# A two-layer latent attention kernel: the second layer's packed queries come through memory, first keys and turned maxima are rearranged

## The chip, the cores and the metric

One NeuronCore of one Trainium2 chip runs the whole program. The metric is the device time of one execution in microseconds (us). The kernel before took 1229.85 us as the median of three executions (1229.53, 1229.85 and 1231.4).

## What is computed

A Perceiver-like network of two layers. The latents `x` are 128 rows of 256; the context is 12,544 rows of 192. Each layer is a cross attention from the latents to the context, a small attention or feed-forward among the latents, and a mixture of experts. What the change touches is the cross attention, in both layers:

```python
q = (query @ Wq + bq)   # 128 x (heads*d); layer 0: 8 heads of 64, no bias; layer 1: 16 heads of 16
k = (key @ Wk + bk)     # 12544 x (heads*d)
v = (value @ Wv + bv)
attn = softmax(q k^T * d**-0.5, axis=-1)
out = attn @ v, then @ Wo + bo
x = x + out
```

with `query` the layer norm of `x` and `key = value = context`.

## The kernel before

The program is written by engine: each of the five engines has one list of instructions (a `@block` function), in an order written out by hand, and the lists are tied by semaphores. Nothing reorders them. SP (the sync engine) and POOL issue all the DMAs, in the order of their lists, so a wait in SP's list holds every later DMA of SP.

**The context** comes in 49 groups of two tiles of 128 keys, 256 KB each. Each cross attention goes over it twice. The first pass makes rough scores and keeps their running maximum for each head and query: half of the scores go from PSUM to VectorE, which takes the maximum into `run` (fp32, line 1359, semaphore `front`), the other half is copied to bf16 by ScalarE (line 489, `half`) and its maximum taken by VectorE in bf16 (line 1364, semaphore `run`). Behind the pass the maxima over the lanes are needed: VectorE casts the bf16 half to fp32 (line 1369), TensorE turns both halves with transposes (`turn_lanes`, line 795), VectorE reduces them (line 1381), a further transpose (line 809) makes a row of them, and SP puts the row in place by a DMA (`max_row`, line 310). The second pass makes the exact scores, with the maximum already subtracted, exponentiates them on ScalarE (layer 0: line 504, layer 1: line 515) and multiplies with the values.

**Layer 1, the beginning.** TensorE keeps itself busy with products that nobody reads (`keep_warm`, line 645; one of them is two records in the trace) while VectorE makes the layer norm; ScalarE gives its root (line 471). Then come two transposes, the copy `xt` (line 1258), the projection of the queries `queries1` (16 products, recorded at line 657, all in PSUM bank 0), then `keys1(0)` (lines 710 to 714), `values1(0)` and `rests1(0)` (line 699). ScalarE copies the keys (line 524), their remainders (line 529) and the values (line 536). VectorE adds the bias to the queries (line 1299, four instructions) and spreads them over block diagonals (line 1303, four instructions), and only then raises `q_diag`, for which TensorE waits before its second keys and its first scores.

**Layer 1, the first pass.** For each group TensorE makes keys, scores of two tiles, remainders and values. POOL splits the raw context group into high and low parts (lines 390 to 397, semaphore `hi1`), and waits for the values of the group two before. SP's list holds, for each group, the load of a context group into one of two buffers (line 273; it waits until POOL is done with the buffer), the store of a group's values to memory (line 290) and the store of a group's keys (line 284, which waits for line 529). ScalarE's copy of keys and values waits until the store of two groups before has landed.

**Layer 1, between the passes.** The second pass has its queries "packed": for each pair of heads 96 rows, three copies of 32. Before the change they are a projection of their own, with columns of Wq repeated on the host: `packed1` (16 products of 128 columns, 32 records at line 657), then eight activations with the bias on ScalarE (line 573) and two more that spread them to the two sides (line 578); VectorE makes the low part (line 1455, two instructions), then copies 32 rows of the first group's keys (`keys_again`, line 1462). The second pass's scores need all of these and `max_row`. ScalarE's first exponential needs its function table (`ACT_TABLE_LOAD`, recorded at the line of the activation it serves).

**Layer 1, the second pass.** SP loads keys and values of three groups ahead (lines 297 and 305). Products with the values are recorded at line 908.

The functions themselves follow.

Of the kernel before, what the change touches and what calls it, by code (L numbers as in the profile page):

```python
# [34 lines left out]
P = 128  # L35
# [29 lines left out]
def xq_offsets(layer):  # L65
# [4 lines left out]
    for name, n in ((("wq", DK * inner), ("wk", nb * QS)) if layer == 0 else  # L70
                    (("wq", DK * 512), ("wqp", DK * PAIRS * P), ("wka", D), ("wkb", D), ("bk", D), ("bv", D), ("bq", UNITS),
                     ("bqp", PAIRS))) + (
# [19 lines left out]
def perceiver(nc, x_in, ctx_in, xq0_in, xq1_in, const_in, la_in, lb_in, ff_in, ex0_in, ex1_in, b1_in, own_in, b2_in, k_mem, v_mem, out):  # L92
    with ExitStack() as stack:
# [28 lines left out]
        minus = sb("minus", [P, P], F32R)  # L122
        probs = sb("probs", [P, W1])
# [139 lines left out]
        def _(sp):  # L263
# [70 lines left out]
            store_keys(1, 1)  # L334
            with sp.Fori(2, GROUPS // 2) as i:
# [22 lines left out]
            sp.wait_ge(sem("q_hi"), 3)  # L358
# [109 lines left out]
        def _(act):  # L468
# [3 lines left out]

            def round_hi(g, slot, first):
# [64 lines left out]
            def pass1(layer):  # L538
# [11 lines left out]
                if layer == 0:  # L550
                    round_hi(0, 0, True)
                else:
                    keep_keys(0, 0, True)
                    keep_rests(0, 0)
                    keep_values(0, 0, True)
# [32 lines left out]
            def cross(layer):  # L588
                root(3 * layer)
# [50 lines left out]
        def _(pe):  # L640
# [1215 lines left out]
```

## Time and profile before

| what | value |
|---|---|
| median of 3 executions | 1229.85 us |
| profiled execution, its own time | 1231.95 us |
| its span, first to last instruction | 1230.0 us |
| TensorE busy | 1178.4 us, 96% |
| VectorE busy | 670.0 us, 54% |
| ScalarE busy | 671.0 us, 55% |
| GpSimd busy | 213.1 us, 17% |
| mean granted TensorE clock | 0.979 of full speed |
| first pass of layer 1 | about 694 to 921 us of the span |
| second pass of layer 1 | about 933 to 1147 us of the span |

Times in the rows are microseconds from the start of the span. "Granted clock" is the share of full speed that TensorE was given in a stretch: 1.00 is 2.4 GHz and 0.50 is 1.2 GHz. Busy time of a matmul is modelled: consecutive ones overlap.

### The profile page before, as it was taken

What the parts mean: (1) busy time and instruction counts of PE and PEld (TensorE: products, weight loads), DVE (VectorE), ACT (ScalarE), POOL (GpSimd) and SP (SyncE); (2) the same over time, 40 slices, a digit from 0 to 9 for tenths busy, and PEclk for the clock granted to TensorE, in tenths of its full rate; (3) what the DMA queues carried; (4) which work ended last, traced back from release to release, by engine and by line L of the source; (5) the groups of instructions that cost most, each with busy time, mean ns of one, the idle gap of its engine ahead of it and who ended that gap; (6) DMA issues with size and microseconds to landing.
All of it is one profiled execution on the core that took longest, in us unless ns stands there. A gap on an engine that the chain in (4) does not pass through costs nothing.

```text
span 1230.0 us, 29349 instructions
## 1 busy us (share of the span) xinstructions
PE 1178.4 (96%) x10142; PEld 945.5 (77%) x10142; DVE 670.0 (54%) x1138; ACT 671.0 (55%) x1092; POOL 213.1 (17%) x312
## 2 busy tenths in 40 slices
PE   6999999999999999999777899999999999999998
PEld 5887777777777777777665688888887888888784
DVE  5999444443444343434753588888885444444442
ACT  2897333333333333333120388788886899988420
POOL 0000100000000000000003377778750110000110
PEclk8999999999999999999979999999998999999989
DMA  3444700010011001000336267667665895555442
GB/s 132 137 138 119 312 26 26 26 34 26 26 27 33 26 26 34 26 26 26 116 116 278 92 225 230 223 221 235 222 219 176 289 303 198 185 184 181 158 168 91
DMA packets 62027, 163.97 MB, mean 133 GB/s; under 512 B 6640, under 2 KB 7088, under 8 KB 56304
## 3 DMA queue, kind: packets, MB, share of 16 engines
q1 hardware_dynamic: 53360, 118.54, 29.4%
q0 software_dynamic: 8640, 45.05, 10.2%
q8 instruction: 19, 0.31, 0.1%
q14 instruction: 8, 0.07, 0.0%
HBM read 124.87 MB, written 38.67 MB: 133 GB/s over the span
## 4 chain that ended last, share of the span: by engine, by line
PE 89%; DVE 7%; DMA 2%; ACT 1%; issue 1%; POOL 0%; DVEq 0%; ACTq 0%
PE ps L657 61%; PE ps L908 8%; PE ps L846 8%; PE ps L645 2%; PE ps L699 2%; DMA ring<-ex_in 2%; PE ps L710 1%; PE ps L714 1%; PE ps L711 1%; PE ps L713 1%; PE ps L712 1%; PE ps L1210 1%; PE ps L1044 0%; PE ps L1066 0%; PE ps L1186 0%
## 5 line engine op out<-in xcount | busy, mean ns | idle before, releaser
L1427 DVE TENSOR_TENSOR wide<-wide,probs 128x1024 f32<-128x1024 f32 x97 | 118.9, 1225 | 264.5 <-ACT probs L504 264.5
L1359 DVE TENSOR_TENSOR wide<-ps,wide 128x512 f32<-128x512 f32 (+1 forms) x196 | 187.1, 954 | 32.7 <-PE ps L657 28.0
L515 ACT ACTIVATE probs<-ps 128x1024 f32<-128x1024 f32 x196 | 190.2, 1023 | 22.5 <-PE ps L657 22.3
L504 ACT ACTIVATE probs<-ps 128x512 f32<-128x512 f32 x196 | 117.2, 598 | 113.0 <-PE ps L657 112.9
L489 ACT CAST wide<-ps 128x512 bf16<-128x512 f32 x294 | 162.4, 587 | 29.9 <-PE ps L657 25.3
L657 PE MATMUL ps<-q_ha,t_ha 128*128 128x512 f32 x392 | 156.9, 400 | 3.8 <-DVE q_le L1287 3.8
L496 ACT COPY v_sb<-ps 128x512 f32<-128x512 f32 x98 | 57.6, 588 | 178.5 <-PE ps L657 178.5
L1364 DVE TENSOR_TENSOR wide<-wide 128x512 bf16<-128x512 bf16 (+1 forms) x196 | 108.6, 554 | 13.4 <-ACT wide L489 3.3
L846 PEld LDWEIGHTS ps<-probs,v_sb 128*64 128x64 f32 x1568 | 83.6, 136 | 34.4 <-ACT probs L504 34.0
L657 PE MATMUL ps<-q_ab,q_hk 128*128 128x512 f32 x392 | 108.0, 397 | 0.0
L846 PE MATMUL ps<-probs,v_sb 128*64 128x128 f32 x1568 | 107.0, 279 | 0.0
L908 PE MATMUL ps<-probs,v_sb 128*32 128x128 f32 x3136 | 106.8, 277 | 0.1
L1415 DVE COPY v_sb<-wide 128x256 f32<-128x256 f32 x98 | 28.9, 295 | 120.9 <-PE ps L908 120.7
L657 PEld LDWEIGHTS ps<-q_ha,t_ha 128*128 128x128 f32 x392 | 75.6, 193 | 21.6 <-DVE q_le L1287 4.3
L908 PEld LDWEIGHTS ps<-probs,v_sb 128*32 128x32 f32 x3136 | 80.2, 110 | 13.5 <-ACT probs L515 0.6
L380 POOL DMA_DIRECT2D wa<-ex_in x4 | 2.1, 530 | 468.5 <-DVE x L1482 464.1
L657 PE MATMUL ps<-q_hk,t_e 65*128 65x512 f32 x196 | 79.1, 404 | 0.0
L657 PE MATMUL ps<-wv_ha,t_ha 128*128 128x512 f32 (+1 forms) x196 | 76.4, 390 | 2.4 <-DVE t_b L1405 2.4
L657 PE MATMUL ps<-q_ab,t_ha 128*128 128x512 f32 x196 | 77.8, 397 | 0.0
L657 PE MATMUL ps<-q_le,t_e 65*128 65x512 f32 x196 | 77.1, 394 | 0.0
L657 PE MATMUL ps<-q_ab,t_b 128*128 128x512 f32 x196 | 76.8, 392 | 0.0
L657 PE MATMUL ps<-q_ha,t_la 128*128 128x512 f32 x196 | 76.6, 391 | 0.0
(374 smaller groups left out, 2235.1 us busy)
## 6 DMA issues: line engine op xcount, KB each, us to landing
raw<-ctx_in SPq DMA_DIRECT2D x147, 256.0 KB, 2.6
k_mem<-q_hk SPq DMA_DIRECT2D x49, 512.0 KB, 3.0
v_mem<-probs SPq DMA_DIRECT2D x49, 256.0 KB, 3.5
wide<-v_mem SPq DMA_DIRECT2D x49, 256.0 KB, 4.3
ring<-ex_in POOLq DMA_DIRECT2D x8, 1152.0 KB, 12.4
q_le<-k_mem SPq DMA_DIRECT2D x17, 512.0 KB, 4.4
q_ab<-k_mem SPq DMA_DIRECT2D x16, 512.0 KB, 4.4
q_hk<-k_mem SPq DMA_DIRECT2D x16, 512.0 KB, 4.5
```

Of the source, the lines that this page charges most:

```text
L489: act.copy(half16[:, c:c + 512], ps[:, back_bank(layer, q) + u, :]).then_inc(sem(f"half{layer}"), 1)
L496: act.copy(v_sb[j][:], ps[:, v_bank[j], :]).then_inc(sem("v_sb0"), 1)
L504: act.activation(probs[:, j * 2048 + u * 512:j * 2048 + (u + 1) * 512], ps[:, s_bank[u], :], ACT.Exp).then_inc(sem("exp0"), 1)
L515: act.activation(probs[:, at:at + 1024], ps[:, bank:bank + 2, :].rearrange("p b n -> p (b n)"), ACT.Exp).then_inc(sem("exp1"), 1)
L645: pe.matmul(ps[:, bank, 0:P], ident, ident, start=True, stop=True)
L657: return pe.matmul(o, l, r, start=(k == 0), stop=(k == n - 1), **more)
L846: last = pe.matmul(ps[64 * (k % 2):64 * (k % 2) + 64, 4, (h // 2) * P:(h // 2 + 1) * P], v_sb[j][:, h * 64:(h + 1) * 64], e, start=(start ...
L908: last = pe.matmul(ps[32 * k:32 * k + 32, 4, u * P:(u + 1) * P], v_sb[j][:, h * 32:(h + 1) * 32], probs[:, j * 2048 + h * P:j * 2048 + (h ...
L1359: dve.tensor_tensor(r, ps[:, b:b + half // 512, :].rearrange("p b n -> p (b n)"), r, ALU.max)\
L1364: dve.tensor_tensor(run16, half16[:, q * half:(q + 1) * half], run16, ALU.max)\
L1415: dve.tensor_copy(v_sb[j][:].rearrange("p (h w) -> p h w", w=32)[:, :, 0:16], v_in[slot][:, j * D:(j + 1) * D].rearrange("p (h d) -> p h d ...
L1427: dve.tensor_tensor(run[:, 0:1024], run[:, 0:1024], e, ALU.add).then_inc(sem("lsum"), 1)
```

## The change

Four things, independent of each other in the code:

1. **Packed queries.** `packed1`, its 2,048 weight columns, its bias columns and the eight activations of line 573 go. VectorE already has the queries in `qt` (bias added and scaled). SP stores 64 rows of `qt` to a new memory tensor `q_mem` (128 KB), waits until it has landed, and reads it back with twelve DMAs of 32 KB (three parts, two sides, two blocks) into `q_all`. These fourteen steps stand in SP's list between the store of group 1's keys and the load of group 4. The two spreading activations stay, over 96 rows. ScalarE also copies the first group's 32 key rows, in place of VectorE; 32 rows of `q_ha` are cleared on VectorE during the experts.
2. **Maxima.** The cast to fp32 of the bf16 maxima goes; TensorE turns them as bf16 with a bf16 identity made at the start, into one bank, and VectorE reduces bf16 from PSUM. Both layers.
3. **First keys.** `keys1(0)` and `rests1(0)` on TensorE, and their two copies on ScalarE, stand ahead of the layer norm of layer 1 in both lists; `keep_warm` ahead of it falls from 11 to 6. The queries go to two PSUM banks and VectorE works them bank by bank, with a semaphore for each; the second keys stand ahead of the wait for the queries, and only the third score of a tile waits for the second bank.
4. **The exponential's table.** `ready(n)`: an exponential of one column that nobody reads, behind each layer's first pass, so that the table is loaded there.

```diff
@@ SP
             store_values(0, 0)
             store_keys(1, 1)
+            sp.wait_ge(sem("q_diag"), 3)
+            sp.dma_start(q_mem.rearrange("n r q -> r n q"), qt[0:CB, :].rearrange("r (n q) -> r n q", n=UNITS))\
+                .then_inc(sem("q_out"), 16)
+            sp.wait_ge(sem("q_out"), 16)
+            for part in range(3):
+                for side in range(2):
+                    to = q_all[part * 32 + side * 16:part * 32 + side * 16 + 16, :]
+                    for b in range(2):
+                        sp.dma_start(to.rearrange("p (u b q) -> p b u q", b=2, q=P)[:, b],
+                                     q_mem[2 * b + side].rearrange("(d u) q -> d u q", u=4)).then_inc(sem("q_in"), 16)
             with sp.Fori(2, GROUPS // 2) as i:
                 load(1, 2 * i, 0, False)
...
@@ ScalarE
+            def ready(n):
+
+                act.activation(stat[:, n, 11:12], stat[:, n, 8:9], ACT.Exp, scale=0.0)
+
...
                 else:
-                    keep_keys(0, 0, True)
-                    keep_rests(0, 0)
                     keep_values(0, 0, True)
...
+                ready(0)
                 groups(act, body)
...
             def pass2_1():
-                act.wait_ge(sem("q_psum"), 3)
-                for u in range(PAIRS):
-                    last = act.activation(q_all[:, u * P:(u + 1) * P], ps[:, 6 + u // 4, (u % 4) * P:(u % 4 + 1) * P],
-                                          ACT.Identity, bias=wx1[:, XQ1["bqp"] + u:XQ1["bqp"] + u + 1])
-                last.then_inc(sem("q_hi"), 1)
-                act.wait_ge(sem("q_hi"), 1)
+                act.wait_ge(sem("q_in"), 12 * 16)
                 for side in range(2):
-                    act.activation(own_columns(q_ha[:], side), q_all.rearrange("p (u q) -> p u q", q=P), ACT.Identity,
-                                   scale=cst[:, CONST["side"] + side:CONST["side"] + side + 1]).then_inc(sem("q_hi"), 1)
+                    act.activation(own_columns(q_ha[0:96, :], side), q_all[0:96, :].rearrange("p (u q) -> p u q", q=P), ACT.Identity,
+                                   scale=cst[0:96, CONST["side"] + side:CONST["side"] + side + 1]).then_inc(sem("q_hi"), 1)
+                act.wait_ge(sem("k_in0"), 16)
+                act.copy(kp[0][AGAIN, :], kp[0][32:64, :].bitcast(F32)).then_inc(sem("q_hi"), 1)
+                ready(3)
...
             def cross(layer):
+                if layer == 1:
+                    keep_keys(0, 0, True)
+                    keep_rests(0, 0)
                 root(3 * layer)
@@ TensorE
-                        last = mm(ps[:, 0, u * P:(u + 1) * P], wx1[:, c:c + P], xt[:, k * P:(k + 1) * P], k, DK)
-                last.then_inc(sem("q_psum"), 1)
-
-            def packed1():
...
+                        last = mm(ps[:, 4 + u // 2, u % 2 * P:(u % 2 + 1) * P], wx1[:, c:c + P], xt[:, k * P:(k + 1) * P], k, DK)
+                    if u % 2 == 1:
+                        last.then_inc(sem("q_psum"), 1)
...
-                turn_x(3 * layer, 3 * layer, xn, fill=(0, 11)[layer])
+                if layer == 1:
+                    pe.wait_ge(sem("out0"), 4)
+                    keys1(0, 0, True)
+                    rests1(0, 0)
+                turn_x(3 * layer, 3 * layer, xn, fill=(0, 6)[layer])
...
+                                if first and t == 0 and n % 2 == 0:
+                                    pe.wait_ge(sem("q_diag"), 2 + n // 2)
...
                 if layer == 1:
-                    keys1(0, 0, True)
                     values1(0, 0, True)
-                    rests1(0, 0)
-                    pe.wait_ge(sem("q_diag"), 2)
+                    keys1(1, 1, False)
...
-                if layer == 1:
-                    pe.wait_ge(sem("k_lo"), GROUPS)
-                    pe.wait_ge(sem("staged"), GROUPS)
-                    packed1()
                 pe.wait_ge(sem(f"front{layer}"), TILES)
-                turn_lanes(range(heads // 2), (2, 4)[layer]).then_inc(sem("lanes_f"), 1)
-                pe.wait_ge(sem("lanes"), layer + 1)
-                turn_lanes(range(heads // 2, heads), (3, 0)[layer]).then_inc(sem("lanes_t"), 1)
+                turn_lanes(heads // 2, (1, 4)[layer], run, ident).then_inc(sem("lanes_f"), 1)
+                pe.wait_ge(sem(f"run{layer}"), TILES)
+                turn_lanes(heads // 2, (3, 0)[layer], half16[:, 2048:2048 + heads * 64], ident16[:]).then_inc(sem("lanes_t"), 1)
@@ VectorE
+                link(dve.tensor_copy(ident16[:], ident))
...
+                for b in range(2):
+                    dve.wait_ge(sem("q_psum"), 2 + b)
...
+                    last.then_inc(sem("q_diag"), 1)
...
-                dve.tensor_copy(run[:, half:2 * half], run16).then_inc(sem("lanes"), 1)
...
-                    dve.wait_ge(sem("q_hi"), 3)
+                    dve.wait_ge(sem("q_hi"), 2)
...
-                    keys_again(0, 0)
                     rounds(dve, body)
...
+            link(dve.memset(q_ha[96:P, :].bitcast(F32), 0.0))
```

## Rows read from the trace of the kernel before

**Rows 1.** The page's part 4: shares of the chain that ended last, by engine.

```profile
PE 89%; DVE 7%; DMA 2%; ACT 1%; issue 1%; POOL 0%; DVEq 0%; ACTq 0%
```

**Rows 2.** Timeline, layer 0 between its passes: start, duration, engine, line, what.

```profile
119.02 0.43 DVE L1369 CAST wide<-wide 128x512 f32<-128x512 bf16 x1
...
128.47 1.28 ACT L504 ACT_TABLE_LOAD   x1
...
129.76 1.32 ACT L504 ACTIVATE probs<-ps 128x512 f32<-128x512 f32 x2
```

**Rows 3.** Timeline, layer 1 from the experts' end to the first scores.

```profile
683.50 2.62 PE L645 MATMUL ps<-cst 128*128 128x128 f32 x22
...
685.09 0.20 ACT L471 ACTIVATE stat<-stat 128x1 f32<-128x1 f32 x1 [4.78 <-DVE stat L1245]
...
687.02 2.05 PE L657 MATMUL ps<-xt,wx 128*128 128x128 f32 x16
...
690.29 0.59 ACT L524 CAST q_hk<-ps 128x512 fp32r<-128x512 f32 x1 [4.99 <-PE ps L714]
...
690.65 3.43 DVE L1303 TENSOR_TENSOR q_ab<-qt,cst 64x512 fp32r<-64x512 f32 x4
...
691.27 0.40 PE L699 MATMUL ps<-q_hk,minus 128*128 128x512 f32 x1
```

**Rows 4.** Timeline: TensorE's scores of the second tile, first pass of layer 1.

```profile
699.30 1.10 PE L657 MATMUL ps<-q_ab,q_hk 128*128 128x512 f32 x4
```

**Rows 5.** Windows: stretch, length, busy time of PE, PEld, DVE, ACT, POOL, clock, DMA.

```profile
695.00:698.30 3.30, 3.30 (x12) 2.82 (x12) 1.23 (x1) 1.61 (x4) 1.09 (x2) 0.50 0.41 154
```

**Rows 6.** Timeline: SP's stores and loads around group 4, POOL's split, TensorE's keys.

```profile
698.87 0.39 SPq L284 DMA_DIRECT2D k_mem<-q_hk  x1
699.62 0.35 SPq L273 DMA_DIRECT2D raw<-ctx_in  x1
...
704.03 0.62 POOL L390 TENSOR_TENSOR t_e<-raw,ones 64x256 fp32r<-64x256 f32 x1 [0.61 <-PE ps L657]
...
707.21 0.74 POOL L397 TENSOR_TENSOR t_b<-raw,t_b 64x256 fp32r<-64x256 f32 x1
...
709.39 0.28 PE L710 MATMUL ps<-t_ha,wk_ha 128*128 128x256 f32 x1
```

**Rows 7.** DMA issues from 690 and from 916 us: count, size, us to landing.

```profile
k_mem<-q_hk SPq DMA_DIRECT2D x6, 512.0 KB, 3.1
raw<-ctx_in SPq DMA_DIRECT2D x6, 256.0 KB, 3.3
...
q_hk<-q_le SPq DMA_DIRECT2D x1, 8.0 KB, 4.4
```

**Rows 8.** Timeline, layer 1 between its passes and into the second.

```profile
921.76 1.22 DVE L1359 TENSOR_TENSOR wide<-ps,wide 128x1024 f32<-128x1024 f32 x1
...
925.64 2.49 DVE L1381 TENSOR_REDUCE sm<-ps 128x8 f32<-128x1024 f32 x2 [1.34 <-PE ps L795]
...
928.50 0.28 DVE L1389 TENSOR_SCALAR m_n<-ps 16x128 fp32r<-16x128 f32 x1 [0.37 <-PE ps L809]
...
929.19 0.54 SPq L310 DMA_DIRECT2D q_ha<-m_n  x1
929.20 2.47 DVE L1455 SCALAR_TENSOR_TENSOR q_ha<-probs,cst,q_ha 32x1024 fp32r<-32x1024 f32 x2 [0.42 <-ACT q_ha L578]
929.83 1.48 SPq L305 DMA_DIRECT2D wide<-v_mem  x3
...
933.06 2.20 PE L657 MATMUL ps<-q_ha,q_le 128*128 128x256 f32 x12 [1.92 <-DVE q_le L1462]
...
933.88 1.28 ACT L515 ACT_TABLE_LOAD   x1 [4.71 <-PE ps L657]
...
941.06 1.08 PE L908 MATMUL ps<-probs,v_sb 128*32 128x128 f32 x32
```

**Rows 9.** Windows, in the columns of rows 5: start of the second pass.

```profile
936.00:940.00 4.00, 3.75 (x39) 3.05 (x40) 0.50 (x2) 2.94 (x4) 0.00 (x0) 0.50 0.22 68
```

More of the change, by code:

```diff
@@ L89, with perceiver @@
 FFW = DK * 1024 + F1T * D
-def perceiver(nc, x_in, ctx_in, xq0_in, xq1_in, const_in, la_in, lb_in, ff_in, ex0_in, ex1_in, b1_in, own_in, b2_in, k_mem, v_mem, out):
+def perceiver(nc, x_in, ctx_in, xq0_in, xq1_in, const_in, la_in, lb_in, ff_in, ex0_in, ex1_in, b1_in, own_in, b2_in, k_mem, v_mem, q_mem, out):
     with ExitStack() as stack:
@@ L744, in scores1 @@
                     else:
-                        if not after:
+                        if not after and not (first and slot == 0):
                             keys1(g + 1, 1 - slot, False)
@@ L791, in cross, with turn_lanes @@
                 scores1(GROUPS - 1, 0, False, True)
-                def turn_lanes(heads, bank):
-                    for n, h in enumerate(heads):
-                        last = pe.transpose(ps[:, bank + n // 4, (n % 4) * P:(n % 4 + 1) * P],
-                                            run[:, h * P:(h + 1) * P], ident)
-                    return last
-                if layer == 1:
-                    pe.wait_ge(sem("k_lo"), GROUPS)
-                    pe.wait_ge(sem("staged"), GROUPS)
-                    packed1()
+                def turn_lanes(n, bank, src, unit):
+                    to = ps[:, bank:bank + 2, :].rearrange("p b n -> p (b n)")
+                    if src is not run:
+                        to = to.bitcast(BF16)
+                    for h in range(n):
+                        last = pe.transpose(to[:, h * P:(h + 1) * P], src[:, h * P:(h + 1) * P], unit)
+                    return last
                 pe.wait_ge(sem(f"front{layer}"), TILES)
-                turn_lanes(range(heads // 2), (2, 4)[layer]).then_inc(sem("lanes_f"), 1)
-                pe.wait_ge(sem("lanes"), layer + 1)
-                turn_lanes(range(heads // 2, heads), (3, 0)[layer]).then_inc(sem("lanes_t"), 1)
+                turn_lanes(heads // 2, (1, 4)[layer], run, ident).then_inc(sem("lanes_f"), 1)
+                pe.wait_ge(sem(f"run{layer}"), TILES)
+                turn_lanes(heads // 2, (3, 0)[layer], half16[:, 2048:2048 + heads * 64], ident16[:]).then_inc(sem("lanes_t"), 1)
                 keep_warm((4, 8)[layer], (5, 3)[layer])
@@ L886, in pairs1 @@
                     if j == 0:
-                        pe.wait_ge(sem("k_again"), KSLOTS * i + slot + 1)
+                        if new and slot == 0:
+                            pe.wait_ge(sem("q_hi"), 3)
+                        else:
+                            pe.wait_ge(sem("k_again"), KSLOTS * i + slot)
                     t = (KSLOTS * i + slot) * GT + j
@@ L1296, in queries1 @@
             def queries1():
-                dve.wait_ge(sem("q_psum"), 2)
-                for u in range(UNITS):
-                    link(dve.tensor_scalar(qt[:, u * P:(u + 1) * P], ps[:, 0, u * P:(u + 1) * P],
-                                           wx1[:, XQ1["bq"] + u:XQ1["bq"] + u + 1], float(HD[1]) ** -0.5, ALU.add, ALU.mult))
                 def diagonal(out, u, rows):
@@ L1305, in diagonal @@
                         cst[rows, CONST["mask4"]:CONST["mask4"] + 4].unsqueeze(2).to_broadcast([n, 4, P]), ALU.mult)
-                for u in range(UNITS):
-                    rows = slice((u % 2) * CB, (u % 2 + 1) * CB)
-                    last = diagonal((q_la, q_b)[u // 2][rows, (u % 2) * 512:(u % 2 + 1) * 512], u, rows)
-                last.then_inc(sem("q_diag"), 1)
+                for b in range(2):
+                    dve.wait_ge(sem("q_psum"), 2 + b)
+                    for u in (2 * b, 2 * b + 1):
+                        link(dve.tensor_scalar(qt[:, u * P:(u + 1) * P], ps[:, 4 + b, u % 2 * P:(u % 2 + 1) * P],
+                                               wx1[:, XQ1["bq"] + u:XQ1["bq"] + u + 1], float(HD[1]) ** -0.5, ALU.add, ALU.mult))
+                    for u in (2 * b, 2 * b + 1):
+                        rows = slice((u % 2) * CB, (u % 2 + 1) * CB)
+                        last = diagonal((q_la, q_b)[b][rows, (u % 2) * 512:(u % 2 + 1) * 512], u, rows)
+                    last.then_inc(sem("q_diag"), 1)
             def value_his(n, va, vb):
@@ L1852 @@
     v_mem = nc.dram_tensor("v_mem", (GROUPS, P, 2 * GK), F32).ap()
-    perceiver(nc, *aps, k_mem, v_mem, out)
+    q_mem = nc.dram_tensor("q_mem", (UNITS, CB, P), F32).ap()
+    perceiver(nc, *aps, k_mem, v_mem, q_mem, out)
     r = run_bass_kernel_spmd(nc, [given], core_ids=[0])
```

36 lines of the change are left out of this document (13 added, 23 removed).

## The prediction, made before the changed kernel was run

> **What bounds the kernel now.** I read the chain that ended last first: TensorE holds 89% of it [rows 1], so what an edit on another engine is worth is only what it takes out of TensorE's idle time. Then I read the timeline at the three handovers that the diff touches, the windows there for the granted clock, and the DMA issues with their landing times. Between the passes of layer 0 (117 to 125 us), at the start of layer 1 (683 to 694) and between its passes (921 to 933) TensorE's useful work waits for VectorE or ScalarE. In the first pass of layer 1 it runs without a gap from 700 us, so a new stall there is lost for good.
>
> **Part A, layer 0 between the passes.** The cast of 0.43 us [rows 2] stands in VectorE's list ahead of two weight copies, both reductions, the maxima's row and the split of the first group, on which TensorE waits. It goes: **-0.4 us**. The turned bf16 half is ready before the second reduction wants it; I take that reduction at its old length. The table load of 1.28 us starts at 128.47, right behind a copy; the two exponentials start at 129.76 [rows 2] and TensorE has work without a gap there, up to products that come at 133.9. `ready(0)` hides what is hidden already: 0. The bf16 identity (one 128x128 copy) falls into VectorE's wait for the first queries: 0. The memset of 32 rows of `q_ha` costs about the 1.8 us of its twin on `q_le`, in a 3.3 us wait of VectorE for the experts' weights: 0. The megabyte less of weights is loaded under layer 0's second pass: 0.
>
> **Part B, the start of layer 1.** *The root.* The first keys take the place of the warming products at 683.50 [rows 3]. Their ten products and the wait for them take 1.4 us (queries end at 689.07, the first key product starts a quarter us earlier, the copy starts at 690.29 [rows 3]): 684.9. Then on ScalarE the copy, 0.59; on TensorE the remainders, 0.4 plus an exposed weight load, 0.5; on ScalarE the copy again, 0.59: 686.65. All this stands ahead of the root in ScalarE's list. And the root needs its table. In rows 2 the load stands right behind the copy that precedes its activation, 10 us after ScalarE was free: loads are not put ahead of copies. So here it no longer runs at 679 under the experts, but behind the second copy: 686.7 to 688.0. The root comes at 688.0 in place of 685.09 [rows 3], **2.9 us later**, and the norm, transposes and queries with it: queries at 689.9 in place of 687.02.
>
> *The banks.* VectorE starts after half of the queries' 2.05 us: at 691.0. Its bias and diagonals took from 689.1 to 694.08 without a pause [rows 3], so now 691.0 to 696.0: 1.9 us later than before. But by then TensorE has done the values, the second keys and two of four scores, which formerly (keys and scores) stood behind this wait. Left are two scores 0.46, remainders 0.25, values 1.2: the second tile's scores start at 697.9, against 699.30 [rows 4]: **-1.4 us**. The old stretch from 695.0 to 698.3 ran at a granted 0.50, 1.2 GHz, all busy [rows 5], behind a 2.5 us gap; at full clock it is 1.6 us shorter. My sum assumes that the new gaps (0.7, 1.4 and 1.1 us, with work between) don't bring the clock down. If they do, this term is +0.2.
>
> *SP's list.* This is the term that decides. The store of group 1's keys was issued at 698.87 and the load of group 4 at 699.62 [rows 6]. Now the store goes at about 698.0, since ScalarE's half-tile copies are a little ahead. Behind it: the store of `qt`, issued at 698.5; its landing; twelve issues; only then the load of group 4. The landing has no row. The nearest is the key store, 3.1 us [rows 7], which it follows on the same queue; ends 2.6 (what is left of that store) and 4.4 (an 8 KB transfer behind a half-megabyte one [rows 7]). An issue: three value loads take 1.48 [rows 8], so 0.49 each; I take 12 x 0.48 = 5.7. Ends: the key store's 0.39 [rows 6], 4.7, and the 0.64 from the maxima's row to the next issue [rows 8], 7.7. So the load of group 4 goes at 698.5 + 3.1 + 5.7 = 707.3, 7.7 us late. It lands in 3.3 [rows 7]; POOL splits it in 3.9 (704.03 to 707.95 [rows 6]): 714.5. TensorE's fourth-group keys stood at 709.39 [rows 6], so now 708.0. The old slack was only 709.39 - 3.9 - 3.3 - 699.62 = 2.6 us. **Stall: +6.4 us** (4 to 9 with the ends). The value store behind that load lands at about 711.5; ScalarE waits for it, but inside the same stall. And a gap like this takes the clock down: behind the 2.5 us gap 3.3 us ran at half speed, so **+1.6 us**.
>
> The Trainium skill (DMA: Bandwidth & Descriptors, section Anatomy of one DMA) gives a software-issued transfer about 2.0 us fixed plus its bytes at 436 GB/s. By that figure, as an estimate, the 128 KB store would land in 2.3 us and the stall would be 0.8 us shorter; this trace's nearest store has 3.1 [rows 7], and no run yet shows it for this shape.
>
> **Part C, layer 1 between the passes.** The packed projection, 3.7 us of TensorE, and eight activations, 2.2 us, go. The last fp32 maximum ends at 922.98 [rows 8]; eight fp32 transposes, 1.1: 924.1; the eight bf16 ones follow. VectorE reduces from 924.1 instead of 925.64 and needs 2.49 [rows 8]; I keep that length, as no row has a reduction of bf16 from PSUM (by the element half of it is the other half's price, below it perhaps 0.6 less). So the row of maxima is ready at 927.3, in place of 928.78, and its DMA is no longer held by ScalarE: 927.3 for 929.19 [rows 8]. ScalarE is free from 921.9: two spreading activations 2.2 (the second ended at 929.17, just ahead of VectorE's low part), a copy of 2,048 columns about 2.0 (twice the 1.02 of a 1,024-column one), the table 1.28: ready at 927.6. VectorE makes the low part from 927.3 in 2.47 [rows 8]: 929.8. The maxima's row must land: it had 3.8 us at most before, in layer 0 2.9, so about 930. TensorE starts at **930.0 in place of 933.06**. The exponential follows its scores directly, 930.7 in place of 935.16, since the table (1.28 [rows 8]) is there. Next limit: the values of the first group, issued at 927.9 and used within 3.1 us before, then `keys_again(1)` behind them on VectorE, 1.2, at 932.6; products need the second exponential, 932.8, anyway. The second pair of products, at 941.06 before [rows 8], then stands at about 935.2: **-5.9 us**. Of these 3.1 are the start, 1.3 the table and 1.5 the clock: 936 to 940 ran at 0.50 [rows 9] behind the 1.9 us gap, which is gone. Against it: without the packed projection TensorE idles 921.4 to 923.0. If that brings the clock down, the warming products ahead of the two waits take twice as long, and the term is -4.3.
>
> **The sum.** -0.4 - 1.4 + 6.4 + 1.6 - 5.9 = **+0.3 us**. The profiled execution took 1231.95 with a span of 1230.0; it lies 2.1 above the median of 1229.85, against which I give the time: 1230.2.
>
> **The rivals.** *R1, SP's detour is hidden.* If small transfers issue and land within the 2.6 to 4 us of slack that group 4 has, stall and clock loss go: 0.3 - 8.0 = -7.7, 1222 us. Half of the stall gives 1226. For it: small data, and all buffers were empty shortly before. Against it: a round trip to memory and twelve issues in one list, with no row under 0.33 us for an issue. 0.2. *R2, the detour is longer and the clock falls with it: slower.* Place: the load of group 4; price: each us of landing or issue beyond 8.8 is a us of TensorE; with the upper ends the stall is 9.2, +2.8. With the low clock at either handover (+1.6 each) it is +3 to +6, 1233 to 1236. It decides as soon as the stall passes 8.5 us, or passes 6.9 with one handover slow. 0.25. *R3, the root's table is loaded ahead of the copies.* Then part B is 1.3 us better: 1228.9. By the Trainium skill (ScalarE activation tables, section Table sets in the compiler and the runtime) the back end places loads per block by the greedy longest run, which would allow that. Rows 2 speak against it. 0.05. *R4, the change does less than it says:* the detour moves the stall but the second pass's start is held by something I hold hidden (values' loads, landing of the row): part C -3, 1233; in R2's share.
>
> **How the numbers follow.** My forecast has 0.5; its own range is 1227.5 to 1232.5. About 0.2% (2.5 us) is what a measurement of this kernel can tell from no change. Of the forecast 0.39 lies within that, 0.04 faster and 0.07 slower; R1 is faster with 0.2; R2 and R4 slower, 0.21 of 0.25, the rest same; R3 same. Faster 0.24, same 0.48, slower 0.28. The range takes half of R1 and most of R2: 1224 to 1235.5.
>
> **What would show it.** The sqrt table load at about 686.7, behind two copies, and the root near 688. VectorE's diagonals in two groups, ending near 696. Twelve issues of SP in a row from about 701.6, load of group 4 near 707, and one stall of TensorE of 4 to 9 us, ended by POOL, then about 3 us at 0.50. No cast at line 1369's place, no table load between the first scores and the first exponential of either second pass, TensorE's second pass starting about 7 us behind the end of the last fp32 maximum (10.1 before). I am wrong if the keys of group 4 don't wait, if the load comes at 679 as before, or if the second pass starts over 1 us from its place relative to the end of the first.

## The result, and the profile after

The changed kernel takes 1232.35 us in the median; beside it on the same chips the kernel before takes 1229.69. The ratio is 1.0028 with a 95% interval of 1.0017 to 1.0038: **slower by 3.4 us** (2.1 to 4.7); the two medians lie 2.7 apart. The forecast was 1230.2, no change that can be measured, with a range of 1224 to 1235.5. The profiled execution took 1231.71 with a span of 1229.9, against 1231.95 and 1230.0 before, so the two single profiles show no difference as wholes. They have to be read stretch by stretch.

The page of the changed kernel: part 1, and the first line of part 4.

```profile
PE 1168.8 (95%) x10100; PEld 935.8 (76%) x10100; DVE 669.6 (54%) x1137; ACT 671.1 (55%) x1087; POOL 212.1 (17%) x312
...
PE 80%; DVE 9%; issue 6%; DMA 2%; ACT 1%; SPq 1%; DVEq 1%; POOL 0%; ACTq 0%; POOLq 0%
```

TensorE was at 89% of the chain [rows 1] and is at 80%. I use four marks, each a distance within one profile: the start of the norm's statistics of layer 1 (before 684.23, after 681.60), the end of the last fp32 maximum of the first pass, the start of the second group of products of the second pass, the end of its last products. From the first mark to the last it is 464.29 us before and 467.62 after, +3.3.

What lies ahead of the first mark is 2.63 us shorter after. Of this 0.33 is layer 0's handover, and 1.90 is layer 0's second pass, as ScalarE's third and last copies of values show, first before, then after:

```profile
136.34 0.59 ACT L496 COPY v_sb<-ps 128x512 f32<-128x512 f32 x1 [1.79 <-PE ps L657]
...
582.84 0.59 ACT L496 COPY v_sb<-ps 128x512 f32<-128x512 f32 x1 [1.79 <-PE ps L657]
```

```profile
136.01 0.59 ACT L510 COPY v_sb<-ps 128x512 f32<-128x512 f32 x1 [1.78 <-PE ps L671]
...
580.61 0.59 ACT L510 COPY v_sb<-ps 128x512 f32<-128x512 f32 x1 [1.78 <-PE ps L671]
```

That is 446.50 us before and 444.60 after, at a granted clock of 1.00 in both from 160 to 580 us. All ten profiles of kernels that hold the change have 444.6, and the three with the old code there (before and the two detours below) have 446.50. So the gain comes with the change; which step brings it no run shows. The remaining 0.4 us is a difference between single profiles: of 13 profiles the first mark lies between 677.94 and 684.90, and the low clock in layer 0 falls at other places (from 20 to 40 us the granted clock was 0.83 before and 0.91 after).

| kernel | root | first pass | second pass starts | second products | first to last mark | median us | ratio to before |
|---|---|---|---|---|---|---|---|
| before | 0.86 | 238.75 | 10.08 | 18.08 | 464.29 | 1229.69 | |
| after | 3.73 | 248.57 | 6.83 | 11.59 | 467.62 | 1232.35 | 1.0028 |
| `spread` | 3.74 | 237.78 | 6.83 | 11.60 | 456.85 | 1221.84 | 0.9929 |
| `keys_behind` | 0.87 | 246.62 | 7.95 | 12.71 | 466.80 | 1232.29 | 1.0024 |
| `detour_alone` | 0.87 | 248.27 | 10.09 | 16.09 | 471.94 | 1236.89 | 1.0064 |
| `detour_six` | 0.86 | 244.55 | 10.08 | 16.09 | 468.10 | 1235.78 | 1.0039 |
| `spread_root_mid` | 1.13 | 235.87 | 7.95 | 12.71 | 456.05 | 1223.03 | 0.9941 |
| `spread_keys_behind` | 0.86 | 237.66 | 6.83 | 11.60 | 456.71 | 1222.64 | 0.9943 |
| `spread_warm` | 1.15 | 236.22 | 7.88 | 12.63 | 456.32 | 1222.67 | 0.9937 |
| `spread_warm_half` | 1.14 | 236.24 | 6.83 | 11.59 | 455.29 | 1219.91 | 0.9918 |

(Root and first pass from the first mark; second pass and products from the end of the last fp32 maximum.) **Part B is 9.82 us longer, part C 6.49 us shorter.**

The two profiles then give -0.33 - 1.90 + 3.33 = +1.1 us for the change, and the measured +3.4 (2.1 to 4.7) is more. The likely cause is the profile of the kernel before: its second products stand at 18.08, while `detour_alone` and `detour_six`, which have the same code at this handover, both have them at 16.09, with a granted clock of 1.00 where the kernel before had 0.50 [rows 9]. If the kernel before mostly runs as the detours do, the sum is +3.1. With 16.09 for 18.08 in the kernel before, such sums for all ten kernels here that have a measured interval (the changed kernel and its variants, and the detours) fall inside it; with 18.08 five of them fall outside. No second profile of the kernel before is there to settle it. The start of the second pass in the windows of `detour_alone`, beside [rows 9]:

```profile
941.00:946.00 5.00, 3.47 (x51) 2.94 (x50) 1.62 (x4) 4.84 (x5) 0.00 (x0) 1.00 0.09 20
```

The timeline of the changed kernel, start of layer 1: start, duration, engine, line, what, and in brackets the idle time before and who ended it.

```profile
681.60 0.43 DVE L1256 BATCH_NORM_STATS2 stat<-x 128x6 f32<-128x256 f32 x1
...
682.25 0.59 ACT L538 CAST q_hk<-ps 128x512 fp32r<-128x512 f32 x1 [5.87 <-PE ps L721]
...
683.43 0.59 ACT L543 CAST q_hk<-ps 128x512 fp32r<-128x512 f32 x1 [0.59 <-PE ps L706]
684.03 1.28 ACT L481 ACT_TABLE_LOAD   x1
...
685.33 0.20 ACT L481 ACTIVATE stat<-stat 128x1 f32<-128x1 f32 x1
```

The two copies of the first keys, then the table, then the root, as in [rows 3] only the root: it comes 3.73 us behind the mark, formerly 0.86. And the stall, in the same timeline:

```profile
695.41 1.08 PE L671 MATMUL ps<-q_ab,q_hk 128*128 128x512 f32 x4
695.55 0.40 SPq L284 DMA_DIRECT2D k_mem<-q_hk  x1
...
695.99 0.72 SPq L336 DMA_DIRECT2D q_mem<-qt  x1
...
698.86 7.61 SPq L343 DMA_DIRECT2D probs<-q_mem  x12
...
706.83 0.37 SPq L273 DMA_DIRECT2D raw<-ctx_in  x1
...
709.78 0.61 POOL L400 TENSOR_TENSOR t_e<-raw,ones 64x256 fp32r<-64x256 f32 x1 [10.28 <-DMA raw<-ctx_in]
...
713.51 0.58 PE L717 MATMUL ps<-t_ha,wk_ha 128*128 128x256 f32 x1 [7.91 <-POOL t_b L407]
```

Read it upward from the last row. TensorE's keys of group 4 wait 7.91 us for POOL; POOL had waited 10.28 for the load; the load was issued behind twelve issues that took SP 7.61 us; these stood behind the store's landing, 698.84. In [rows 6] the load of group 4 followed the key store by 0.75 us, here by 11.3. ScalarE's wait for the value store, in the waits of 700 to 722 us (us, times, longest), lies inside the same stall:

```profile
ACT probs L550 <- DMA v_mem<-probs: 5.9, 1, 5.9
```

The windows, in the columns of [rows 5]: the idle stretch, and what the clock does behind it.

```profile
708.00:713.40 5.40, 0.00 (x0) 0.00 (x0) 0.94 (x1) 1.56 (x3) 3.46 (x5) 0.65 0.99 319
713.40:717.00 3.60, 3.48 (x13) 3.29 (x14) 0.09 (x1) 0.59 (x1) 3.22 (x6) 0.50 0.64 243
717.00:720.90 3.90, 3.90 (x17) 3.48 (x16) 2.04 (x3) 2.15 (x4) 0.69 (x3) 0.63 0.24 91
720.90:725.60 4.70, 4.70 (x31) 4.00 (x30) 3.89 (x5) 3.80 (x8) 3.69 (x6) 1.00 0.44 149
```

Group 4 runs at 0.50 and takes 7.43 us from its keys to the next group's (713.51 to 720.94), where a group takes 4.65: 2.8 us more. The DMA issues of 694 to 722 us, with the median time to landing:

```profile
raw<-ctx_in SPq DMA_DIRECT2D x4, 256.0 KB, 3.4
...
probs<-q_mem SPq DMA_DIRECT2D x12, 32.0 KB, 2.1
q_mem<-qt SPq DMA_DIRECT2D x1, 128.0 KB, 2.9
```

Between the passes of layer 1, the changed kernel's timeline:

```profile
928.95 1.22 DVE L1373 TENSOR_TENSOR wide<-ps,wide 128x1024 f32<-128x1024 f32 x1
...
930.23 1.09 PE L810 MATMUL ps<-cst,wide 128*128 128x128 f32 x8 [1.86 <-DVE wide L1373]
...
931.15 0.61 PE L810 MATMUL ps<-ident,wide 128*128 128x128 bf16 x8
931.42 2.49 DVE L1395 TENSOR_REDUCE sm<-ps 128x8 f32<-128x1024 f32 x2 [0.66 <-PE ps L810]
...
933.06 1.28 ACT L485 ACT_TABLE_LOAD   x1
...
934.49 2.46 DVE L1469 SCALAR_TENSOR_TENSOR q_ha<-probs,cst,q_ha 32x1024 fp32r<-32x1024 f32 x2
...
937.00 1.70 PE L671 MATMUL ps<-q_ha,q_le 128*128 128x256 f32 x12
...
941.76 1.08 PE L921 MATMUL ps<-probs,v_sb 128*32 128x128 f32 x32
```

The last maximum ends at 930.17, the second pass starts at 937.00 and its second products at 941.76. In [rows 8] the same three stand at 922.98, 933.06 and 941.06. The reduction over fp32 and bf16 took 2.49 us, exactly as over fp32 alone.

### The profile page after: what moved, and what is told of

Its sections match the earlier page's. It is cut to its first block, busy times and chain, and to the rows that moved or that the text cites. A ratio compares the mean times of both kernels' runs of the same rounds, so it can differ in the third digit from the quotient of the medians.

```text
span 1229.9 us, 29275 instructions
## 1 busy us (share of the span) xinstructions
PE 1168.8 (95%) x10100; PEld 935.8 (76%) x10100; DVE 669.6 (54%) x1137; ACT 671.1 (55%) x1087; POOL 212.1 (17%) x312
## 4 chain that ended last, share of the span: by engine, by line
PE 80%; DVE 9%; issue 6%; DMA 2%; ACT 1%; SPq 1%; DVEq 1%; POOL 0%; ACTq 0%; POOLq 0%
PE ps L671 53%; PE ps L856 8%; PE ps L921 8%; PE ps L706 2%; DMA ring<-ex_in 1%; DVE wide L1373 1%; PE ps L659 1%; DVE wide L1378 1%; PE ps L717 1%; PE ps L721 1%; PE ps L719 1%; PE ps L718 1%; PE ps L720 1%; PE ps L1057 1%; PE ps L1223 1%
```

## The experiments

**Four about the detour.** *`spread`*: the changed kernel, but the load of group 4 goes ahead of the wait for the store, and each of the next twelve group steps of SP's list carries one of the twelve loads.

```diff
-            sp.wait_ge(sem("q_out"), 16)
-            for part in range(3):
...
-            with sp.Fori(2, GROUPS // 2) as i:
+            for i in range(2, 8):
+                load(1, 2 * i, 0, False)
+                if i == 2:
+                    sp.wait_ge(sem("q_out"), 16)
+                store_values(2 * i - 3, 1)
+                pack(2 * i - 4)
...
```

> The changed kernel, but the load of group 4 stands ahead of the wait for the query store, and the twelve packed-query loads stand one by one in the next twelve group steps of SP's list, each behind a value store. Theory 1, SP's detour starves group 4: TensorE's 7.9 us idle before its keys of group 4 is gone and the half-clock stretch behind it (1.6 us) too, so 9.5 us less than the changed kernel: 1222.9 us, ratio to before about 0.994. Rival, the lateness comes from the first keys standing ahead of the norm's root (and its table load behind two copies), the detour being hidden otherwise: no more than 1 us moves, 1231 to 1232.

Measured: 0.9929 (0.9909 to 0.9949), its median 10.5 us below the changed kernel's (by the two ratios 12, give or take 3). The first pass is 10.79 us shorter, everything else on the table stands to 0.01 us. SP's queue in its timeline:

```profile
692.37 0.70 SPq L336 DMA_DIRECT2D q_mem<-qt  x1
693.11 0.64 SPq L273 DMA_DIRECT2D raw<-ctx_in  x1
695.29 0.33 SPq L290 DMA_DIRECT2D v_mem<-probs  x1
695.66 0.62 SPq L343 DMA_DIRECT2D probs<-q_mem  x1
```

The loads cost SP 0.6 us apiece still, but one in a group step of 4.65 us is free. So stall and clock come from the place of the fourteen steps in SP's list, not from the traffic. The edit does two things, the load ahead of the wait and the loads one to a step; which of them would do alone no run shows.

*`keys_behind`*: the changed kernel with `keys1(0)` and `rests1(0)`, and their copies, behind the queries again (warming products 11).

```diff
-                if layer == 1:
-                    pe.wait_ge(sem("out0"), 4)
-                    keys1(0, 0, True)
-                    rests1(0, 0)
-                turn_x(3 * layer, 3 * layer, xn, fill=(0, 6)[layer])
+                turn_x(3 * layer, 3 * layer, xn, fill=(0, 11)[layer])
```

> The changed kernel with the first keys and their remainders (and ScalarE's two copies) put back behind the queries, the warming products back at 11; queries still bank by bank. Theory 1: the root comes 2.9 us earlier again, as do the queries; VectorE's diagonals end 2.9 us earlier, and TensorE's own work up to the third score (values, keys, remainders, second keys, two scores) just fits ahead of that: 2 to 2.9 us faster than the changed kernel, with the stall at group 4 as long as there (7 to 8.5 us): about 1229.8. Rival, the first keys' place costs the whole slow-down: 3.4 us or more faster than the changed kernel and the stall at group 4 shorter than 4 us. If the first keys' new place gains what it was made for, this kernel is slower than the changed one.

Measured: 1.0024 (1.0012 to 1.0036), as the changed kernel, so the 2 to 2.9 us did not come. The root is back at 0.87 and the first pass 1.95 us shorter, with a stall of 7.7, but the handover behind it is 1.12 us longer, at the lower clock.

*`detour_alone`* and *`detour_six`*: the kernel before, with only SP's store, wait and loads added, twelve, or six with one side alone, into a place that nobody reads. No other step of the change is in them.

```diff
+            sp.wait_ge(sem("q_diag"), 2)
+            sp.dma_start(q_mem.rearrange("n r q -> r n q"), qt[0:CB, :].rearrange("r (n q) -> r n q", n=UNITS))\
+                .then_inc(sem("q_out"), 16)
+            sp.wait_ge(sem("q_out"), 16)
+            for part in range(3):
+                for side in range(2):
+                    to = spare[part * 32 + side * 16:part * 32 + side * 16 + 16, :]
...
```

> The kernel before, with nothing changed but SP's detour: query store, wait, twelve loads into a spare place that nobody reads; its own packed projection is kept. Theory 1: load of group 4 at 710, landed 712.9, split by 716.7 against keys of group 4 at 709.4: stall 7.3 us plus 1.6 of half clock, 8.9 us slower than before, 1238.6, ratio 1.007. Rival, the detour is hidden by the buffers: ratio 1.000 to 1.002.

> As the run with the detour alone, but six loads instead of twelve. Theory 1: each load takes 0.64 us of SP's list, so the stall is 3.8 us shorter: 3.5 plus up to 1.6 of half clock, 4 to 5 us slower than before, ratio 1.0033 to 1.004. Rival: as before within 2 us.

Measured: 1.0064 (1.0042 to 1.0086) and 1.0039 (1.0022 to 1.0056); first passes 9.5 and 5.8 us longer than before. The waits of TensorE for POOL, from 700 to 725 us, first of `detour_alone`:

```profile
PE ps L721 <- POOL t_b L408: 7.5, 1, 7.5
```

and of `detour_six`:

```profile
PE ps L721 <- POOL t_b L408: 3.6, 1, 3.6
```

Six issues are 3.9 us of stall: **0.65 us of TensorE for each**, which is their pitch in the timeline, 7.62 / 12 = 0.64. In both the first pass is 2 us longer than the stall alone makes it, which is the clock: the group behind the stall takes 7.0 and 7.1 us, where a group takes 4.65.

**Two about the start.** *`spread_root_mid`*: on `spread`, a small square root ahead of the copies, so that the table comes early, and the root between the two copies.

```diff
                 if layer == 1:
+                    act.activation(stat[:, 3, 11:12], stat[:, 0, 8:9], ACT.Sqrt)
                     keep_keys(0, 0, True)
-                    keep_rests(0, 0)
                 root(3 * layer)
+                if layer == 1:
+                    keep_rests(0, 0)
```

> This is `spread` with one small activation that asks for the root's table ahead of the first keys' copies, and with the root between those two copies instead of behind both. My theory of the late root: of its 2.9 us, 1.3 are the table load, which stands directly ahead of the root and therefore behind the copies, and about 1.2 are the remainders' products and second copy. Then the table load runs about 5 us earlier, the root comes 2.4 us sooner than in `spread` (about 1.3 us after the norm's statistics' start mark plus nothing of the old 3.7), the diagonals end 2.4 us earlier, and the third score no longer waits 1.3 us for them: first pass 1.5 to 2.4 us shorter, about 1220. Rival: VectorE's diagonals were not what held the pass; the third score's wait moves on to the remainders' or values' copies, whose ScalarE copy now comes later, and the first pass is as long as in `spread` (within 0.5 us): 1221.8. A second rival: the table is loaded again for the root wherever it stands, and nothing changes.

Measured: the table load runs at 678.68, five us ahead of the mark, the root comes 1.13 behind it, the first pass is 1.91 us shorter. But the time is 0.9941 (0.9919 to 0.9964), not below `spread`: 1.12 us came back at the handover. Its timeline there:

```profile
919.80 1.92 PE L824 MATMUL ps<-cst,wide 128*128 128x128 f32 x8 [1.86 <-DVE wide L1387]
921.51 1.06 PE L824 MATMUL ps<-ident,wide 128*128 128x128 bf16 x8
922.36 2.47 PE L673 MATMUL ps<-cst 128*128 128x128 f32 x16
```

The eight fp32 turns take 1.92 where the changed kernel has 1.09, the bf16 ones 1.06 for 0.61: 1.2 GHz, behind the same 1.86 us of idle time behind which the changed kernel ran at full clock.

*`spread_keys_behind`*: on `spread`, the edit of `keys_behind`.

> This is `spread` with the first group's keys and remainders behind the queries again, as in the kernel before. Between the changed kernel and `keys_behind` this took 1.95 us off the first pass of layer 1, but 1.1 came back at the handover behind it, which ran at the lower clock. In `spread` the stall is gone, so if the early keys cost by themselves (the late root), the first pass is 1.5 to 2.5 us shorter than in `spread`, 235.3 to 236.3, and the time about 1220 to 1221. Rival: what `keys_behind` won was only a longer stall's start, that is group 4's load came at the same time whatever stood before it; then with the stall gone the first pass is as long as in `spread`, or longer by the 1.4 us that the prediction gave to work moved ahead of the wait: 1222 to 1223.

Measured: 0.9943 (0.992 to 0.9965), a first pass of 237.66, as in `spread`: the rival held, but not for its reason. The second tile's scores start 11.86 us behind the first mark against 13.85 in `spread`, so the 2 us are won at the start. They are lost again: 0.6 in the first groups, with waits of 0.77 for a copy of the remainders and 0.33 for POOL, and the rest over the pass, where two groups take 9.36 us for 9.30 in `spread`, with TensorE busy all the time. POOL's timeline, about 787 us:

```profile
785.72 0.61 POOL L412 TENSOR_TENSOR t_e<-raw,ones 64x256 fp32r<-64x256 f32 x1 [0.46 <-POOL t_b L419]
786.29 0.61 POOL L413 TENSOR_TENSOR t_ha<-raw,ones 128x256 fp32r<-128x256 f32 x1
786.86 1.11 POOL L414 TENSOR_TENSOR t_b<-raw,ones 128x256 fp32r<-128x256 f32 x1
788.05 0.74 POOL L416 TENSOR_TENSOR t_la<-raw,t_ha 128x256 fp32r<-128x256 f32 x1
788.87 1.09 POOL L419 TENSOR_TENSOR t_b<-raw,t_b 64x256 fp32r<-64x256 f32 x1
```

and 20 us of its windows, then the same of `spread`:

```profile
743.00:763.00 20.00, 20.00 (x127) 16.77 (x126) 17.16 (x17) 16.20 (x31) 17.79 (x23) 1.00 0.70 229
```

```profile
743.00:763.00 20.00, 20.00 (x126) 17.26 (x125) 16.32 (x17) 16.32 (x31) 16.07 (x23) 1.00 0.69 224
```

POOL is busy 17.8 of 20 us instead of 16.1: two of its five operations last 1.1 us, where in `spread` one does, and each long one lies beside VectorE's bf16 maximum (786.49 and 788.67 here). POOL no longer waits for TensorE. That this is what holds the pace I read from the two profiles; it is not shown, since TensorE is busy throughout and no run took it away.

**Two about the handover.** Each was executed once (1222.84 and 1221.58 us), so they have no interval, and only distances in their profiles are read. *`spread_noready3`*: `spread` without `ready(3)`.

> This is `spread` without the small exponential ahead of the second pass of layer 1. If the table is worth what the prediction said, it is loaded behind the first scores, the first exponential of the second pass starts 1.3 us later, and the second pair of products stands about 12.9 us behind the end of the last fp32 maximum, where `spread` has 11.6. Rival: the products wait for the values or for VectorE's repeated keys as well, and then it stands within 0.4 us of 11.6.

Measured: the second products stand 12.86 us behind the last maximum, 1.26 later than in `spread`. Here the table's 1.28 us are worth what they last.

*`spread_f32turn`*: `spread` with the cast and the fp32 turn of the bf16 half put back, in both layers.

> This is `spread` with the bf16 half of the maxima cast to fp32 again in both layers and turned as fp32. Theory: the cast is 0.43 us of VectorE, whose list decides between the passes of layer 0, so there the distance from the last maximum to the first split goes from 6.3 to about 6.7 us. In layer 1 VectorE waits for the turned first half anyway, and the bf16 reduction was no faster than the fp32 one: the cast lies in that wait, and the start of the second pass moves by 0 to 0.1 us. Rival: turning eight tiles in fp32 takes TensorE 1.09 us instead of 0.61, the second reduction waits for it, and both handovers are 0.5 to 0.9 us longer.

Measured: between the passes of layer 0, from the last fp32 maximum to the end of the last split, 6.63 us against 6.29 in `spread`: the cast. In layer 1 the second pass starts 8.76 us behind the maximum, 1.93 later, far from my 0.1. Its timeline:

```profile
919.55 0.69 DVE L1393 CAST wide<-wide 128x1024 f32<-128x1024 bf16 x1
...
920.30 1.53 PE L820 MATMUL ps<-cst,wide 128*128 128x128 f32 x8 [0.24 <-DVE wide L1393]
921.41 3.22 PEld L671 LDWEIGHTS ps<-cst 128*128 128x128 f32 x16
921.62 3.20 PE L671 MATMUL ps<-cst 128*128 128x128 f32 x16
```

The turns wait 0.24 us for the cast and are fp32 (eight take 1.09 at full clock, bf16 0.61); then the clock falls, and sixteen warming records take 3.20 us where `spread` has 2.00. They stand ahead of the turn of the row in TensorE's list, so warming products hold up real work. How much of the 1.93 is the cast without the clock I can't separate in this profile; the second reduction starts 0.5 us later.

**Three for the clock at the handover.** *`spread_warm`*: `spread_root_mid` with warming products in TensorE's idle 1.9 us ahead of the turns.

```diff
+                if layer == 1:
+                    pe.wait_ge(sem("staged"), GROUPS)
+                    keep_warm(14, 7)
                 pe.wait_ge(sem(f"front{layer}"), TILES)
```

> This is `spread_root_mid` with 14 more warming products on TensorE, in its idle 1.9 us between the last scores of layer 1's first pass and the turned maxima. Theory: the 1.1 us that the handover cost more in `keys_behind` and `spread_root_mid` are the eight turns and sixteen warming products at 1.2 GHz, and the lower clock there follows from that idle time. With it filled the granted clock stays 1.00 through the handover, the second pass starts 6.8 us behind the last fp32 maximum, not 8.0, and with the first pass at 235.9 us the stretch from the norm to the end of the second pass is 454.9 us, 1.9 under `spread`: about 1220 us. Rival: the clock falls anyway, because what it follows is not this gap; then the second pass starts 8.0 us behind and the time is `spread`'s within 0.1%. A second rival: the warming products end late or hold the turned maxima up, and the start moves back by what they overrun, up to 0.5 us.

Measured: 0.9937 (0.9918 to 0.9957). The granted clock is 1.00 through the handover, but `keep_warm(14)` is 28 records in the trace and 3.29 us, longer than the gap. The turns start 1.1 us late: the second rival, larger than I allowed.

*`spread_again`*: `spread` once more, beside it.

> This is `spread` once more, beside `spread_warm` on the same chip, so that a difference of 0.15% can be read. Theory: ratio 0.993 to the kernel before, a first pass of 237.8 us, and the second pass starting 6.8 us behind the last fp32 maximum; `spread_warm` lies 1.9 us below it. Rival: the handover's clock is chance in this kernel too, and the start is 8.0 us behind in this profile.

Measured: 0.9944 (0.9929 to 0.9959), with the same marks as `spread` to 0.05 us (first pass 237.75, start 6.83, to the last mark 456.80). At the same code the handover's clock was the same twice.

*`spread_warm_half`*: seven in place of fourteen.

> This is `spread_warm` with 7 warming products in place of 14, which took 3.29 us where the gap is 1.9; by that row seven take 1.65. Theory: they fit into the gap and keep the granted clock at 1.00 through the handover, so the turned maxima start at once (about 0.05 us behind the last fp32 maximum), the second pass starts 6.8 us behind it, and with the first pass at 235.9 us the stretch from the norm to the end of the second pass is 454.9 us, against 456.8 in `spread`: about 1.9 us less, 1220 to 1221 us. Rival: the 0.25 us of idle time that is left, or the waits further on, bring the clock down all the same, and the stretch is 456.0 us as in `spread_root_mid`.

Measured: **1219.91 us, 0.9918** (0.9898 to 0.9938), the fastest median. Its timeline:

```profile
918.11 1.72 PE L673 MATMUL ps<-cst 128*128 128x128 f32 x14
920.13 1.09 PE L824 MATMUL ps<-cst,wide 128*128 128x128 f32 x8 [0.30 <-DVE wide L1390]
921.06 0.61 PE L824 MATMUL ps<-ident,wide 128*128 128x128 bf16 x8
```

Turns at full clock, second pass 6.83 behind, 455.29 us to the last mark, 1.56 under `spread`. The intervals of the two ratios overlap, so the times alone don't show it faster than `spread`; the stretch, which two profiles of `spread` repeat to 0.05 us, is what tells them apart.

## Where the prediction held, and the main term that it sized too small

The time lies inside the stated range of 1224 to 1235.5, but the outcome with the largest chance, no change (0.48), did not come; slower (0.28) did. The mechanism was named and happened: one stall of TensorE ended by POOL, behind twelve issues of SP, then a stretch at 0.50. The sum of +0.3 came out too low by the sizes of part B's two last terms. The result is near what rival R2 described, slower by about 3 us, though by other shares than R2 gave. R1, the hidden detour, did not happen: the stall was 7.9 us. R4 gives a like time, but not for its reason: the second pass's start was not held, it came 6.83 us behind the last maximum for a forecast 7.

- *SP's list, +6.4, measured 7.9.* Three sizes. The landing of the store: taken 3.1, measured 2.85. The issue: taken 0.48 from three value loads [rows 8], measured 0.637, so 7.6 for twelve, and 8.0 to the load behind them, and not 5.7; this alone is 2.3 us. **This choice between the rows failed**: the range of 0.39 to 0.64 was right, and I chose by the nearest row's kind (a load to SBUF), where the other end, 0.64, turned out right. The load's landing, to POOL's start: taken 3.3, measured 2.95. The recorded ends of this term are also added wrongly: landing 2.6 to 4.4 and issues 4.7 to 7.7 make a stall of 5.0 to 9.8 (6.5 in the middle), not 4 to 9, and with the upper ends R2 is at +3.6, not +2.8. From the first mark the load of group 4 was forecast at +23.1 and stands at +25.2, the keys at +30.3 and +31.9.
- *The clock behind it, +1.6, measured 2.8.* I took the price from a stretch of 3.3 us behind a 2.5 us gap [rows 5]. Behind 7.9 us the low clock held to about 720, 6.5 us; the group behind it took 7.4 us, and behind stalls of 7.7 (`keys_behind`), 7.5 and 3.6 (the detours) it took 6.5, 7.0 and 7.1, so the length of the stall does not set the loss. R2's condition was a stall over 8.5 us, or over 6.9 with one handover slow; the stall stayed below 8.5, no handover of the changed kernel was slow, and the clock behind the stall took the rest.
- *The store's landing and the page.* The trace's nearest store had 3.1 [rows 7]; this shape landed in 2.85 here, 2.97 in `detour_alone`. The Trainium skill (DMA: Bandwidth & Descriptors, section Anatomy of one DMA) gives a fit for a software-issued transfer, by which 2.3 is the estimate; this one is issued by SP, and the measured value lies between 2.3 and 3.1. The landing is 0.25 of the difference, the issues 2.3.
- *The start, -1.4, measured -1.3* (second tile's scores 15.07 behind the mark before, 13.81 after). The root was forecast 2.9 us later and came 2.87 later. In `spread_root_mid` 2.6 of these come back and shorten the first pass by 1.9. What was left there is the third score's wait for the diagonals, 1.29 us.
- *R3, the table ahead of the copies,* did not happen: the load stands directly ahead of the root, 684.03, behind both. By the Trainium skill (ScalarE activation tables, section Table sets in the compiler and the runtime) placing by the longest run would allow an earlier one; here no row shows it, and only an activation of the same table further up moved it.
- *Part C, -5.9, measured -6.49,* and near only in part by its reasons. Start 3.1, measured 3.25; table 1.3, measured 1.26 by `spread_noready3`; the rest 2.0, the clock, sized 1.5. The cause that I gave for this last one, the 1.9 us gap ahead of the second pass, does not hold: `detour_alone` and `detour_six` have the old handover with that same gap and start (10.09 and 10.08), ran at a granted 1.00 through it, and reached their second products at 16.09, not 18.08. So 2 of the 6.5 us belong to how the clock fell in that profile of the kernel before, whether by build or by execution, and not to the change, which is worth 4.5 here. That the term came out near was luck. My caveat, that the clock could fall in TensorE's new idle time and cost 1.6, did not come true in the changed kernel; it did in `keys_behind` and `spread_root_mid`, for 1.1.
- *Part A, -0.4, measured -0.33* (118.65 to 125.27 before, 117.45 to 123.74 after). `ready(0)`'s table load stands at 117.01 under the pass's end, worth nothing that the profiles show, as said.
- *A reduction of bf16 from PSUM at the length of fp32*: right, 2.49 us for both kinds.

- *Layer 0's second pass, no term, measured -1.90.* The prediction gave the smaller weights that are loaded there 0, and named nothing else; all ten profiles with the change show the gain, and its cause is open.

The sum of the prediction's terms with measured sizes is -0.3 - 1.3 + 7.9 + 2.8 - 6.5 = +2.6. The first pass has 0.4 more that no row of mine carries (its pace, 9.30 us for two groups against 9.29 before, makes 0.3 of it): +3.0. This agrees with the measured 3.4 only because two things that the sum has wrong cancel: the 1.9 us of layer 0's second pass are missing, and part C counts 2.0 us of clock that are not the change's. With both it is +3.1; the first is shown by thirteen profiles, the second argued from the detours.

## What to carry to other kernels

A wait and a dozen small DMAs in the list of the engine that also feeds the bound stage cost the sum of the landing and of every issue, less the slack of the next load; put the feeding load ahead of the wait and strew the rest one to a step, and the same traffic is free (10.5 us here). Give every issue in such a list the dearest pitch of the rows when its shape has no row. And sum up a change by distances between marks within one profile, over every stretch, those without a step of the change too, and profile the kernel before more than once: the same spans hid +9.8, -6.5 and -1.9 us.

## What was not expected of the hardware

- One DMA of 32 KB read in pieces from memory holds SP 0.64 us when twelve follow each other, and 0.65 us by the two detours' stalls; plain loads of 256 KB in the same kernel show 0.35 to 0.47 (in `spread` one has 0.64, right behind the store of `qt`).
- The clock does not follow the idle gap alone: behind the same 1.86 us gap at one place the turns ran at 2.4 GHz in the changed kernel and `spread`, and at 1.2 GHz in `keys_behind` and `spread_root_mid`. Filling the gap kept 1.00 in both kernels that did. Each kernel was profiled once, `spread` twice with the same clock, so whether the build or the execution decides is open.
- At 1.2 GHz the warming products themselves become the delay, where they stand ahead of real work (in `spread_f32turn` 3.20 us for 2.00).
- An earlier start can put POOL and VectorE in another phase to each other: one more of POOL's operations beside VectorE's bf16 maximum took 1.1 instead of 0.6 us. In the same kernel the pass gave back the 2 us it had won; that the one caused the other is not shown.
- TensorE's pace in layer 0's second pass, busy all the time at a granted 1.00, is 9.26 us for two copies of values in every kernel with the change and 9.30 without it. No run shows why.
